# The state product of a linear-attention chunk: three passes of rounded halves in place of one plain float32 product

## The reference, cut to what matters

```python
xc = chunked(v * dt[..., None])
G = jnp.cumsum(gc, axis=-1)
scores = jnp.einsum('bhnid,bhnjd->bhnij', qc, kc)
y_intra = jnp.einsum('bhnij,bhnjd->bhnid', scores * decay, xc)
k_dec = kc * jnp.exp(Glast - G)[..., None]
cstates = jnp.einsum('bhnjd,bhnje->bhnde', k_dec, xc)
# scan over chunks: state = state * chunk_decay + cstates
y_inter = jnp.einsum('bhnid,bhnde->bhnie', qc * jnp.exp(G)[..., None], prev)
```

## Time and profile before

| | |
|---|---|
| median of 3 runs | 1835.56 us (1832.38 to 1835.94) |
| the profiled execution, own time | 1833.96 us |
| its span, first to last instruction | 1832.2 us |
| granted TensorE clock, mean | 0.994 of full |
| busy: PE / DVE / POOL / ACT | 1791.7 / 1242.5 / 709.9 / 665.8 us |
| chunk states on PE, share of the chain that ended last | 4.4% |

### The profile page before, as it was taken

How to read it: one execution, slowest core, us unless ns; L and a number is a source line. 1 busy time by engine, 2 the same in 40 slices (tenths; PEclk the granted TensorE clock), 3 DMA queues, 4 the chain that set the end, 5 groups by cost and what they waited for, 6 DMA issues and landing times.

```text
span 1832.2 us, 27509 instructions
## 1 busy us (share of the span) xinstructions
PE 1791.7 (98%) x8728; PEld 1457.4 (80%) x8728; DVE 1242.5 (68%) x2321; ACT 665.8 (36%) x2151; POOL 709.9 (39%) x757
## 2 busy tenths in 40 slices
PE   7998999999999999999999999999979999999998
PEld 5787888888888888888888888888757888888886
DVE  5235888888888888888888888888864333333332
ACT  3432444344344444443434434443543121112121
POOL 2223555455545555555545554655401101010101
PEclk9999999999999999999999999999989999999999
DMA  5233333423323322333332333322564232222321
GB/s 185 87 104 94 108 95 101 116 86 111 116 84 107 121 87 80 114 110 92 98 116 86 111 114 87 109 90 85 173 210 138 77 99 78 95 88 84 96 77 46
DMA packets 145952, 190.30 MB, mean 104 GB/s; under 512 B 9104, under 2 KB 79760, under 8 KB 145808
## 3 DMA queue, kind: packets, MB, share of 16 engines
q1 hardware_dynamic: 145808, 188.58, 34.0%
HBM read 141.89 MB, written 46.66 MB: 103 GB/s over the span
## 4 chain that ended last, share of the span: by engine, by line
PE 86%; DMA 2%; DVE 1%; ACT 1%; issue 0%; SPq 0%; POOL 0%; ACTq 0%; DVEq 0%; POOLq 0%
PE p_proj L85 28%; PE p_kept L85 14%; PE p_tok L1337 9%; PE p_kept L1337 8%; PE p_y L798 6%; PE p_score L85 5%; PE p_y L797 5%; PE p_cst L783 4%; PE p_qa L85 3%; PE p_f L1520 2%; DMA w_raw<-z_scratch 1%; PE p_f L1531 1%; PE p_tok L766 1%; DMA w_raw<-in_wo_t 0%; DMA out_dram<-q 0%
## 5 line engine op out<-in xcount | busy, mean ns | idle before, releaser
L85 PE MATMUL p_proj<-shared,wq_hi 128*128 128x512 f32 x744 | 273.6, 429 | 0.0
L114 POOL TENSOR_TENSOR q<-rope_a,rope_b 128x512 f32<-128x512 f32 x128 | 164.9, 1288 | 267.7 <-DVE rope_b L106 267.7
L1064 ACT ACTIVATE square<-p_y 128x128 f32<-128x128 f32 x512 | 134.5, 278 | 263.7 <-PE p_y L798 261.7
L798 PE MATMUL p_y<-v_tok,probs 128*128 128x128 f32 x1024 | 182.1, 275 | 0.0
L85 PE MATMUL p_proj<-wg_hi,shared 128*128 128x512 f32 x528 | 178.2, 418 | 0.0
L85 PE MATMUL p_kept<-wg_hi,shared 128*128 128x512 f32 x560 | 176.6, 396 | 0.0
L85 PEld LDWEIGHTS p_proj<-shared,wq_hi 128*128 128x128 f32 x744 | 139.8, 188 | 45.3 <-issue 14.8
L939 DVE SCALAR_TENSOR_TENSOR z<-p_y,srstd,gate 128x128 f32<-128x128 f32 x512 | 143.7, 343 | 37.5 <-issue 24.5
L1039 ACT ACTIVATE probs<-g_row,stab 128x128 f32<-128x128 f32 x512 | 164.3, 409 | 9.2 <-POOL g_row L1153 9.2
L1752 POOL TENSOR_TENSOR var<-mv,eps 128x1 f32<-128x1 f32 x16 | 3.0, 190 | 418.2 <-DVE mv L1602 418.2
L1171 POOL TENSOR_TENSOR srstd<-svar,mhalf 128x4 f32<-128x4 f32 x128 | 157.4, 1230 | 10.0
(11 more groups left out here) (225 smaller groups left out, 4211.5 us busy)
## 6 DMA issues: line engine op xcount, KB each, us to landing
g_row<-g_scratch SPq DMA_DIRECT2D x128, 256.0 KB, 4.3
z_scratch<-z_st SPq DMA_DIRECT2D x256, 128.0 KB
w_raw<-z_scratch SPq DMA_DIRECT2D x62, 512.0 KB, 6.6
e_row<-e_scratch SPq DMA_DIRECT2D x96, 256.0 KB, 4.0
w_raw<-in_wq_t SPq DMA_DIRECT2D x16, 512.0 KB, 7.2
w_raw<-in_wg_t SPq DMA_DIRECT2D x16, 512.0 KB, 6.0
v_tok<-v_scratch SPq DMA_DIRECT2D x32, 256.0 KB, 2.9
w_raw<-in_wo_t SPq DMA_DIRECT2D x12, 512.0 KB, 5.4
```

The lines of the kernel that those rows point to most:

```text
L85: mm = pe.matmul(out, lhs[a], rhs[e], start=(i == 0 and j == 0), stop=(i == len(pairs) - 1 and j == 2))
L114: pool.tensor_tensor(out, keep["rope_a"][:, s, :], keep["rope_b"][:, s, :], ALU.add).then_inc(keep["roped"], 1)
L798: mm = pe.matmul(p_y[c % 2][:, h, :], probs[:, c % 2, h, :], v_tok[:, b % 2, c, :], start=(c == 0), stop=True)
L1064: s = act.activation(square[:, h, :], p_y[c % 2][:, h, :], ACT.Square, scale=2.0 / float(np.sqrt(D)), accum_out=ssum[:, c, h:h + 1])
```

## The change

A chunk's state becomes a `wide` product. k_tok and xw are therefore split in halves. `save_k` now writes the high half of k_tok; DVE subtracts the low half from the bank (`k_tok_low`). POOL writes the weighed values into one buffer `xw_raw`, ACT rounds it to `xw_hi` (`xw_high`), and POOL subtracts to `xw_lo` (`xw_low`). Each of the three has one buffer. `make_xw` of a step's chunk 0 moves to the end of the step before it. The core of the diff:

```diff
-        k_tok = sb("k_tok", [P, NC, D])
+        k_tok = [sb(f"k_tok_{e}", [P, NC - 1, D], F32R) for e in ("hi", "lo")]
-        xw = sb("xw", [P, 2, HG, D])
+        xw_raw = sb("xw_raw", [P, HG, D])
+        xw = [sb(f"xw_{e}", [P, HG, D], F32R) for e in ("hi", "lo")]
@@ PE, chunk_state
-                pe.matmul(p_cst[:, :, :], k_tok[:, c, :], xw[:, c % 2, :, :], start=True, stop=True).then_inc(cst_done, 1)
+                wide(pe, p_cst[:, :, :], [([w[:, c, :] for w in k_tok], [w[:, :, :] for w in xw])]).then_inc(cst_done, 1)
@@ DVE: at the end of first(), and in step() between turn_z(n, 2) and make_gate(g, b, n, 3)
+            def k_tok_low(n):
+                dve.wait_ge(tok_hi_set, n + 1)
+                dve.tensor_tensor(k_tok[1][:, :, :], p_tok[:, 0:NC - 1, :], k_tok[0][:, :, :].bitcast(F32),
+                                  ALU.subtract).then_inc(tok_saved, 1)
@@ ACT
-                act.activation(k_tok[:, 0:NC - 1, :], p_tok[:, 0:NC - 1, :], ACT.Copy).then_inc(tok_saved, 1)
+                act.activation(k_tok[0][:, :, :], p_tok[:, 0:NC - 1, :], ACT.Copy).then_inc(tok_hi_set, 1)
+            def xw_high(n, c):
+                act.wait_ge(xw_raw_set, 3 * n + c + 1)
+                wait_ge(act, cst_done, 3 * n + c)
+                act.activation(xw[0][:, :, :], xw_raw[:, :, :], ACT.Copy).then_inc(xw_hi_set, 1)
 first():    make_decay(0, 0, 0)
+            xw_high(0, 0)
 last_step(): make_tanh(g, b, n, c)
+                    if c < NC - 2:
+                        xw_high(n, c + 1)
 step():     make_decay(n, b, 1)
+                xw_high(n, 1)
 ...
             make_decay(n, b, 2)
+                xw_high(n, 2)
 ...
                     save_k(n + 1)
+                    xw_high(n + 1, 0)
@@ POOL
-                wait_ge(pool, cst_done, 3 * n + (c - 1 if c else 0))
+                wait_ge(pool, xw_set, 3 * n + c)
-                pool.tensor_tensor(xw[:, c % 2], v, w, ALU.mult).then_inc(xw_set, 1)
+                pool.tensor_tensor(xw_raw[:, :, :], v, w, ALU.mult).then_inc(xw_raw_set, 1)
+            def xw_low(n, c):
+                pool.wait_ge(xw_hi_set, 3 * n + c + 1)
+                pool.tensor_tensor(xw[1][:, :, :], xw_raw[:, :, :], xw[0][:, :, :].bitcast(F32), ALU.subtract).then_inc(xw_set, 1)
 first():    mask(0, 1)
+                make_xw(0, 0, 0, 0)
 step():
-                make_xw(g, n, b, 0)
+                xw_low(n, 0)
 ...
                 make_xw(g, n, b, 1)
+                xw_low(n, 1)
 ...
                 make_xw(g, n, b, 2)
+                xw_low(n, 2)
 ...
                     mask(n + 1, 1)
+                    make_xw(g, n + 1, b + 1, 0)
                 if group_ahead(g) and b == B - 2:
                     w_low(wq, wq_hi, g + 1, q_split[1])
```

More of the change, by code:

```diff
@@ L563, in attention_stage @@
         squares_set, tok_saved = sem("squares_set"), sem("tok_saved")
-        masked_set, xw_set = sem("masked_set"), sem("xw_set")
+        masked_set, xw_raw_set, xw_hi_set, xw_set = sem("masked_set"), sem("xw_raw_set"), sem("xw_hi_set"), sem("xw_set")
+        tok_hi_set = sem("tok_hi_set")
         q_hi_set, q_lo_set, k_hi_set, k_lo_set = sem("q_hi_set"), sem("q_lo_set"), sem("k_hi_set"), sem("k_lo_set")
@@ L884, in first @@
                 q_low(0, 0, 0)
+                k_tok_low(0)
+            def k_tok_low(n):
+                dve.wait_ge(tok_hi_set, n + 1)
+                dve.tensor_tensor(k_tok[1][:, :, :], p_tok[:, 0:NC - 1, :], k_tok[0][:, :, :].bitcast(F32),
+                                  ALU.subtract).then_inc(tok_saved, 1)
             def make_gate(g, b, n, c):
@@ L1007, in step @@
                 turn_z(n, 2)
+                if ahead(n):
+                    k_tok_low(n + 1)
                 make_gate(g, b, n, 3)
```

## The result

The changed kernel takes 1822.01 us, the median of 6 runs (1818.88 to 1824.83), against 1835.68 us for the kernel before in 6 runs beside them (1832.38 to 1836.28). The ratio is 0.9929, with a 95% interval of 0.9915 to 0.9943: 0.7% faster. The forecast was 1822. The profiled execution took 1818.88 us, its span 1817.0.

What follows compares the result with a forecast made beforehand. PE's own instruction stream was taken as the bound. Products gain 14.9 us; start 1.9, clock 0.8 and last step 0.3 lose 3.0; net -11.9 from 1833.96 gives 1822 us, range 1817 to 1831.

Steps and rivals of the forecast that it cites:

- Part 1, the product: Chunk state: three rounded passes at 0.70 us replace a plain product at 0.86, gaining 0.16 us each, 14.9 for 93.
- The low bound: Chunk state's three passes cost 0.77 us if the first is held as in the scores behind `mix`'s plain products.
- Four passes for true FP32: Chunk state: four passes become three, saving one pass of 0.233 us each, 22.4 us in all.
- Part 2, the turns: Between steps, chunk 0's split halves are ready before PE, by 0.6 to 1.1 and about 1 us; cost 0.
- rival A: Chunk 0's k_tok_low or subtraction late at most turns; 0.4 us at 31 turns gives 1834.5 us; chance 0.08.
- Part 3, contention: In the attention stage, POOL's subtractions may slow DVE, at most 58 us more DVE work; cost to the end 0.
- rival B: Each POOL subtraction holds up DVE 1.2 us, 112 us for 93; DVE becomes the bound: 1882 us; chance 0.04.
- Part 4, the start: At the first chunk state, multiply, round and subtract in a row make PE wait 1.9 us longer (1.6 to 2.5).
- The clock term: At the start, the longer idle may bring back the low clock: 0 or 1.6 us, half taken, 0.8.
- Part 5, the last step: In the last step, ACT's rounding before its opening copies delays what follows: 0.3 us taken, 0 to 1.9.
- The sum of -11.9: Whole kernel: 14.9 us gained less 3.0 lost, against the profiled execution's 1833.96 us.

Runs made afterwards that it cites:

- the repeat: The changed kernel run again with no edit, compared with the kernel before: 1821.96 us, ratio 0.9934.
- the run with the late k_tok_lo: The changed kernel with an unused sum over 2048 columns on DVE before each k_tok_low: 1834.72 us, ratio 1.0003 to the kernel before.

## Why the prediction was right, point by point

The parts held, at the sizes below. That the time came out within 0.1 us of 1822 is luck. The forecast took some 12 us off the 1833.96 of one execution; the medians differ by 13.7 us and start from 1835.68, and the two differences of some 1.7 us cancel.

- **Part 1, the product.** 0.16 us for each, taken; 0.161 measured over 92. The low bound, 0.77 us for the three passes, didn't occur. How the 0.86 comes about shows in PE's starts in the kernel before:

```profile
1289.94 1.02 PE L783 MATMUL p_cst<-xw,k_tok 128*128 128x512 f32 x2
1290.40 0.79 PE L85 MATMUL p_proj<-shared,wq_hi 128*128 128x512 f32 x1
1291.03 0.39 PE L85 MATMUL p_proj<-shared,wq_lo 128*128 128x512 f32 x1
```

The plain product's own two records take 0.46 us, and the projection's first pass then holds PE for 0.63 us in place of 0.23. Nearly half of the price stood behind the product, in its neighbour's record, and the distance in the chain had both. The loader has a row to match, in the kernel before and with the plain product on split operands:

```profile
PEld p_proj L85 <- issue: 44.5, 186, 0.2
```

Loads behind a plain product waited 0.24 us, 186 times, twice for each of 93 products. The row is absent after. Four passes for true FP32 (the Trainium skill, FP8 and Floating Point Precision, section TensorE Precision Notes) would have given an estimated 22.4 us in all; the trace's 0.86 us stood against it, and 15 was measured.

- **Part 2, the turns.** Margins of 0.6 to 1.1 and 1 us were forecast, 0.58 and 0.68 found, at the low edge, since the subtraction took 2.29 us there, beside DVE's own half of wq_lo, and the multiplication ahead of wq_lo 1.47 us, not 1.03. Counted to the load, as the deadline is, they are 0.35 and 0.45. Cost 0, as taken. But one added operation of 1.0 us turned this into rival A and took the whole gain, so the rival was nearer than its reading, 0.6 us to spare and seven turns, had it.
- **Part 3, contention.** 0 for the end, as taken. DVE's busy time over the full steps, from the second scores to the last step's first, before and after (us, then busy of PE, PEld, DVE, ACT, POOL):

```profile
164.65:1303.70 1139.05, 1139.05 (x5689) 927.50 (x5688) 976.47 (x1867) 478.23 (x1819) 614.71 (x660) 1.00 0.34 101
164.30:1288.53 1124.23, 1124.23 (x5782) 944.45 (x5780) 1005.39 (x1898) 533.47 (x1911) 748.26 (x752) 1.00 0.34 102
```

It rose by 29 us, not 19: k_tok_low is 31 x 0.52 = 16 of it, and the rest are operations that got longer. Summed by operation, which counts twice where neighbouring records overlap, q_lo has 8.3 us more, wg_lo 4.6 and wq_lo 4.4. DVE's half of wq_lo (ns min/median/max), before and after, and at the turn shown above:

```profile
L866 DVE TENSOR_TENSOR wq_lo<-w_raw,wq_hi x7: 2720/2728/2732, 263.5 to 1153.7; 128x1024 fp32r<-128x1024 f32 x7
```

```profile
L869 DVE TENSOR_TENSOR wq_lo<-w_raw,wq_hi x7: 3345/3360/3371, 261.9 to 1140.6; 128x1024 fp32r<-128x1024 f32 x7
```

```profile
554.81 3.36 DVE L869 TENSOR_TENSOR wq_lo<-w_raw,wq_hi 128x1024 fp32r<-128x1024 f32 x1
```

DVE's half starts 0.1 us behind POOL's half and ends at 558.17, 1.08 us behind POOL's end at 557.09; the same form takes 1.22 us where nothing disturbs it (wg_lo before). POOL's subtraction starts at 557.04 and ends 1.16 us behind DVE, where it takes 1.30 alone. So the two took turns, each held until the other was done. This agrees with the exclusive lock that blocks the loser for the whole instruction (the Trainium skill, SBUF — State Buffer, section SBUF: two separate sides). Before, DVE's half began 0.72 us behind POOL's (560.23 against 559.51) and was held for that much less: its 0.63 us come from where it starts, not from the subtraction. What kept rival B's 112 us away is how seldom the two meet: of the 93 subtractions in the full steps, seven meet wq_lo and take 2.3 us themselves, seven hold DVE's wg_lo (1.88 us in place of 1.22), and the others run beside operations that read a bank, or beside none of this kind, at 1.3 us.

- **Part 4, the start.** +1.9 was taken for the wait, 2.52 - 1.16 = 1.36 us found. From the multiplication's start to the product it is 3.10 us, 157.07 - 153.97, against 1.53 before, 157.28 - 155.75: 1.57 more, where I had counted from the multiplication's end and so 0.3 too much; and counted from the first scores, POOL was free 0.2 us earlier. The clock term of 0.8 was a mean of two cases, and the runs have both: 1.00 behind the wait in the changed kernel, 0.57 in the one with the multiplication put back, at 1.43 us more. So in the profiled execution this term was 0, inside the bounds of 0 and 1.6. How often the changed kernel pays it, only its two traces say: neither does.
- **Part 5, the last step.** +0.57, where 0.3 was taken, and +1.07 in the repeat, both inside 0 to 1.9. That ACT, held up ahead of its opening copies, makes the wait on qs longer fits the run that moves the rounding behind them; that this sets the last step's length is not shown.

The sum of -11.9 stands against -14.82 + 1.22 + 0.57 = -13.0 in the trace. Term by term: the products gave 15.0 for 14.9, the start's wait 1.36 for 1.9, the clock 0 for 0.8, the last step 0.57 for 0.3. The largest error is the clock's 0.8.

## What to carry to other kernels

When an engine's stream sets the time, price an operation by the distance between starts in the chain of waits, and ask of each feeder how long before the *load* of its product it is ready: here 0.35 us of margin stood between a gain of 0.7% and none. A slightly late operand may not show in PE's own list of waits; look in that of PEld. Take margins along a whole in-order queue, not one by one. Where only a product's last pass reads the late operand, its wait could stand in front of that pass; no run here tried it.

## What the runs showed of the hardware that was not expected

- A late operand, even one that isn't loaded, holds the load of the pass that waits for it. It costs PE 0.40 us with no idle time shown (above), and a wait of 0.28 us shown as such costs 0.55: the scores around the turn stand 11.22 us apart in place of 10.67.
- Two subtractions with both operands in SBUF, on DVE and POOL, run one behind the other, not side by side: the turn above shows both directions, 3.36 us on DVE in place of 1.22, and then 2.29 on POOL in place of 1.30.
- Whether a wait brings the low clock isn't told by its length alone. At the first chunk state, waits of 2.20, 2.48, 2.52 and 2.52 us left the stretch from 158 to 162 us at 1.00, and 2.27, 2.77, 3.17 and 3.59 had 0.57, 0.57, 0.60 and 0.70 there. In the middle of the stage, waits of 3.0 us were followed by it six times of seven, waits of 1.75 us five times of seven, and the seven of 1.44 us in the run with the late k_tok_lo never.
- An exponentiation of 128x4 on POOL takes 1.01 us in the median, 2.00 at most, and the multiplication of 128x512 takes 1.04. It is the operation and not the size: an addition of 128x4 (svar) takes 0.2 in the median.
